# Moving the output writes of the last stage from POOL's DMA queue to SP's

## The reference

```python
xn = _layernorm(x, axis=-1)
x = x + _L0_attn_ref(xn, wq, wkv_a, wkv_b, wo) + _L0_ffn_ref(xn, router_w, gate_w, up_w, down_w)

def _L0_attn_ref(x, ...):            # 16 heads, 128 plain and 64 rotary columns
    ...
    attn = jax.nn.softmax(scores, axis=-1)
    o = jnp.einsum('bhqk,bkhd->bqhd', attn, v).reshape(b, s, H * VD)
    return o @ wo

def _L0_ffn_ref(x, ...):             # 16 experts of 768, the two best of each row count
    ...
    h = jax.nn.silu(g) * u
    expert_out = jnp.einsum('ebtf,efd->ebtd', h, down_w)
    out = jnp.einsum('ebtd,bte->btd', expert_out, combine)
    return out
```

## Time and profile before

| what | value |
|---|---|
| runs of the kernel before | 7406.59, 7946.9, 7163.06 us (median 7406.59) |
| the profiled execution | 7154.16 us |
| its span, slowest core (core 0) | 7152.6 us |
| spans of the 8 cores | 7116.0 to 7152.6 us |
| PE busy | 5868.2 us, 82% |
| DVE busy | 2477.7 us, 35% |
| POOL busy | 341.8 us, 5% |
| DMA queue q0 (POOL) | 490336 packets, 233.66 MB |
| DMA queue q1 (SP) | 19120 packets, 136.32 MB |

### The profile page before, as it was taken

One profiled execution on the slowest core, in us unless ns is written; L12 is line 12 of the kernel. 1 busy time (PEld: TensorE's weight loads), 2 busy tenths in 40 slices (PEclk: granted clock), 3 DMA queues, 4 the chain that ended last, 5 costly groups with the idle time before them and its releaser, 6 DMA issues.

```text
span 7152.6 us, 76524 instructions; the slowest of 8 cores (7116.0 to 7152.6 us)
## 1 busy us (share of the span) xinstructions
PE 5868.2 (82%) x28475; PEld 2792.7 (39%) x28992; DVE 2477.7 (35%) x4485; ACT 817.9 (11%) x1975; POOL 341.8 (5%) x377
## 2 busy tenths in 40 slices
PE   1677657777777778999999999999999999999900
PEld 1334323433343433444444444444444444444400
DVE  5445324554545443313322331332233123213334
ACT  2022102212221220000000000000000000000000
POOL 0000000000000000000000000000000000000000
PEclk9866676677667758999999999999999999999955
DMA  2311241022013105242233324233332423333165
GB/s 94 40 13 16 60 143 15 10 90 41 10 26 98 17 1 136 24 53 36 37 35 42 42 24 53 36 38 34 42 42 24 53 36 39 32 42 41 12 240 229
DMA packets 509816, 374.91 MB, mean 52 GB/s; under 512 B 468880, under 2 KB 470928, under 8 KB 486928
## 3 DMA queue, kind: packets, MB, share of 16 engines
q0 software_dynamic: 490336, 233.66, 24.2%
q1 hardware_dynamic: 19120, 136.32, 5.1%
HBM read 457.83 MB, written 83.89 MB: 76 GB/s over the span
## 4 chain that ended last, share of the span: by engine, by line
PE 75%; DVE 7%; DMA 6%; ACT 3%; issue 3%; ACTq 2%; DVEq 1%; POOL 0%; SPq 0%; POOLq 0%
PE psG L946 18%; PE psU L952 18%; PE psD L969 18%; PE psA L586 3%; PE psA L664 3%; DMA rb<-scr 3%; ACT probs L871 3%; PE psA L671 3%; PE psAV L701 2%; PE psAV L646 2%; PE psA L576 2%; ACTq L876 2%; PE psTa L633 2%; DMA xw<-x 2%; DVE colM L770 1%
## 5 line engine op out<-in xcount | busy, mean ns | idle before, releaser
L946 PE MATMUL psG<-xnT,gb 128*128 128x512 bf16 x6024 | 1381.5, 379 | 24.8 <-DMA ub<-uw 18.5
L952 PE MATMUL psU<-xnT,ub 128*128 128x512 bf16 x6022 | 1379.9, 379 | 6.4
L969 PE MATMUL psD<-db,hT 128*128 128x512 bf16 x6018 | 1324.4, 379 | 24.5 <-DVE hT L1007 16.9
L1007 DVE TENSOR_TENSOR hT<-sgt,psU 128x512 bf16<-128x512 f32 x384 | 264.1, 688 | 2407.3 <-PE psU L952 2407.3
L1021 DVE SCALAR_TENSOR_TENSOR acc<-psD,comb,acc 128x512 bf16<-128x512 f32 x960 | 721.2, 751 | 544.4 <-PE psD L969 544.4
L946 PEld LDWEIGHTS psG<-xnT,gb 128*128 128x128 bf16 x6144 | 601.4, 98 | 744.8 <-issue 21.0
L969 PEld LDWEIGHTS psD<-db,hT 128*128 128x128 bf16 x6144 | 596.4, 97 | 752.5 <-issue 201.1
L952 PEld LDWEIGHTS psU<-xnT,ub 128*128 128x128 bf16 x6144 | 601.2, 98 | 724.9
L994 ACT ACTIVATE sgt<-psG 128x512 f32<-128x512 f32 x384 | 229.3, 597 | 3680.0 <-PE psG L946 3679.9
L664 PE MATMUL psA<-kns,qn 128*128 128x512 bf16 (+3 forms) x560 | 249.5, 490 | 308.4 <-ACT probs L871 203.6
L871 ACT ACTIVATE probs<-psA,colD 128x512 bf16<-128x512 f32 (+3 forms) x640 | 391.6, 620 | 937.5 <-PE psAV L646 472.2
(11 more groups left out here) (135 smaller groups left out, 2980.5 us busy)
## 6 DMA issues: line engine op xcount, KB each, us to landing
scr<-stage SPq DMA_DIRECT2D x64, 1024.0 KB, 4.0
gb<-gw POOLq DMA_DIRECT2D x96, 512.0 KB, 6.3
ub<-uw POOLq DMA_DIRECT2D x96, 512.0 KB, 8.3
db<-dw POOLq DMA_DIRECT2D x16, 3072.0 KB, 19.5
rb<-scr SPq DMA_DIRECT2D x32, 1024.0 KB, 12.7
rb<-scr POOLq DMA_DIRECT2D x32, 1024.0 KB, 10.6
xbuf<-x SPq DMA_DIRECT2D x16, 1024.0 KB, 5.1
xw<-x SPq DMA_DIRECT2D x16, 1024.0 KB, 7.0
```

Source lines behind the costliest of these rows:

```text
L946: i = t.matmul(ps_g[:], gb[sl][:, dc * 128:(dc + 1) * 128], xnt(dc)[:, tb * 512:(tb + 1) * 512], start=(dc == 0), stop=(dc == ND - 1))
L952: i = t.matmul(ps_u[:], ub[sl][:, dc * 128:(dc + 1) * 128], xnt(dc)[:, tb * 512:(tb + 1) * 512], start=(dc == 0), stop=(dc == ND - 1))
L969: i = t.matmul(ps_d[:], hT[:, fc * 2048 + tc * 128: fc * 2048 + (tc + 1) * 128], db[:, fc * 2048 + dcol * 512: fc * 2048 + (dcol + 1) * 51 ...
L1007: i = v.tensor_tensor(out=hT[:, fc * 2048 + tb * 512: fc * 2048 + (tb + 1) * 512], in0=sgt[k % 2][:], in1=psU[k % 2][:], op=ALU.mult)
```

## The change

The output writes go from POOL's instruction stream to SP's. In SP's loop the write of tile tc - 1, with its wait for the last addition of that tile, stands in front of the loads of `rb[0]` and `rb[1]` for tile tc; the write of the last tile follows the loop, and SP and no longer POOL waits for the last two writes. In POOL's loop only the loads of `rb[2]` and `rb[3]` are left, each with its wait for the third addition of the tile before. VectorE's instructions, the buffers and the bytes moved are the same.

```diff
@@ SP @@
                     for tc in range(NT):
                         if tc >= 1:
+                            wait(sy, ("madd", tc - 1, 4))
+                            i = sy.dma_start(out[(tc - 1) * 128:tc * 128, :], ost[(tc - 1) % 2][:])
+                            sems[f"dOUT{(tc - 1) % 2}"].inc(i, 16)
+                            mark(("outw", tc - 1), sems[f"dOUT{(tc - 1) % 2}"])
+                        if tc >= 1:
                             wait(sy, ("madd", tc - 1, 0))
                         sy.dma_start(rb[0][:], scr[0][tc * 128:(tc + 1) * 128, :]).then_inc(
                             sems[f"dMRG{tc % 2}"].h, 16)
...
                         i = sy.dma_start(rb[1][:], scr[1][tc * 128:(tc + 1) * 128, :])
                         sems[f"dMRG{tc % 2}"].inc(i, 16)
                         mark(("mld", tc, 0), sems[f"dMRG{tc % 2}"])
+                    wait(sy, ("madd", NT - 1, 4))
+                    i = sy.dma_start(out[(NT - 1) * 128:NT * 128, :], ost[(NT - 1) % 2][:])
+                    sems[f"dOUT{(NT - 1) % 2}"].inc(i, 16)
+                    mark(("outw", NT - 1), sems[f"dOUT{(NT - 1) % 2}"])
+                    sy.wait_ge(sems["dOUT0"].h, sems["dOUT0"].n)
+                    sy.wait_ge(sems["dOUT1"].h, sems["dOUT1"].n)
 
@@ POOL @@
                         i = g.dma_start(rb[3][:], scr[3][tc * 128:(tc + 1) * 128, :])
                         sems["dMISC"].inc(i, 16)
                         mark(("gld", tc, 0), sems["dMISC"])
-                        wait(g, ("madd", tc, 4))
-                        i = g.dma_start(out[tc * 128:(tc + 1) * 128, :], ost[tc % 2][:])
-                        sems[f"dOUT{tc % 2}"].inc(i, 16)
-                        mark(("outw", tc), sems[f"dOUT{tc % 2}"])
-                    g.wait_ge(sems["dOUT0"].h, sems["dOUT0"].n)
-                    g.wait_ge(sems["dOUT1"].h, sems["dOUT1"].n)
```

## The result

The changed kernel is slower: 1.012 times the kernel before, with a 95% interval of 1.0093 to 1.0147, which is 67 to 105 us on 7154. The profiled execution took 7243.43 us, against 7154.16 before. The ratio leaves out executions in which the cores of a die ran at a lower clock than the others; the plain medians (7233.09 us of 9 executions, 7284.82 of 10 of the kernel before) contain some.

The account below looks back on a forecast made before the run. Bound taken: the merge's transfers and adds in series, 356.1 us. Losing SP's prefetch adds 14 steps by 1.3 us, 18 us, and 4.3 us for the fifteenth: 7154 + 22 = 7176 us, range 7138 to 7225.

Parts of the forecast that it names:

- The mechanism: In the merge, SP's loads of rb0/rb1 lose their one-tile prefetch, outweighing POOL's loads issued 3.0 us earlier: +22 us, chance 0.66.
- The transfer term: All five transfers of a merge tile, 5.24 MB, keep their measured 15.3 us early and 13.4 us late.
- The wake-up: In each merge tile, 0.1 us between the end of the transfer and the first add.
- A third reading: SP's queue takes about 2 us from issue to data when nothing else runs, read from the loads of tile 1.
- rival (c): In the merge, POOL's and SP's queues don't overlap: transfer 17.0 us a tile, +42 us, 7219 us; chance 0.09.
- A transfer of over 17 us: Sign that the forecast is wrong: a merge tile's transfer over 17 us, where 13.4 to 15.3 us were expected.
- The sum: 14 merge steps at 1.3 us, 18 us, plus 4.3 us for the fifteenth, end of kernel 0: +22 us, 7176 us.
- Its upper end: Queues that don't overlap at all, transfer 17.0 us in 16 tiles: 7219 us, with 6 us of margin 7225.
- The skill's rates: About 358 GB/s for each core of a streaming HBM pair, an estimated 14.6 us of transfer in all tiles.
- The 4 us in which SP's queue stayed behind a busy POOL queue: SP's queue starts 4.3 to 6.4 us after L1087's start, before POOL's runs dry at 7.2: no hole.

Follow-up runs that it names:

- e1_loads_first: Changed kernel with SP issuing the loads of rb0/rb1 first and the output write behind them; 0.9907 times the kernel before, profiled at 7083 us.
- e3_no_prefetch: Kernel before with SP's loads of rb0/rb1 waiting for the last add of the tile before, not the first; 1.0096 times the kernel before.
- e2b_pool_late: Changed kernel with POOL's loads of rb2/rb3 waiting for the last add of the tile before, not the third; 1.0034 times the kernel before.
- e4_no_writes: Changed kernel without the output writes of tiles 0 to 13, waits and loads otherwise as they were; profiled execution 7142.63 us.
- e5_sbuf_source: Changed kernel with the merge's loads of rb0 to rb3 reading pieces of xnT in SBUF instead of HBM; 1.0041 times the kernel before.
- e6_write_behind: Changed kernel with SP, still after the last add, issuing the loads of rb0/rb1 before the output write; 1.0019 times the kernel before.

## Why the prediction was right and wrong

**The mechanism.** Right. The prefetch is gone, all 16 first adds wait for rb0/rb1, the second add waits for nothing, POOL's issues start 0.37 us after the last add begins (0.42 forecast), and there is no short last step on core 2 (24.1 us). e1_loads_first and e3_no_prefetch, which give the prefetch back and take it alone, show that this and not the write's place is the cause.

**The tile.** Forecast for an undisturbed tile: 1.27 + 13.4 + 0.1 + 7.5 = 22.3 us. Measured on core 2: 1.4 + 14.5 + 1.2 + 7.3 = 24.4. Two terms were mis-sized by 1.1 us each, and these are the steps of the sum that failed for a core by itself.

The transfer term. I took "the measured 15.3 and 13.4, since those are the same 5.24 MB with the same kinds of packets on the same two queues". It was the order that was not the same. In the kernel before the write goes first and alone, and its slow stretch is about 2 us long (229 GB/s). In the changed kernel POOL's loads are under way when the write is issued, and the slow stretch is 5 us long at 303 GB/s. e2b_pool_late, where the write is first again, has 13.6 us from packet to packet against 14.6; e4_no_writes puts the price of the write behind POOL's loads at 3.8 us instead of 2.5.

The wake-up. I put 0.1 us between the end of the transfer and the add, and 1.2 were needed: 0.7 us in which the engines stop one after the other, and 0.5 us from the end of the last packet to the add (0.43 to 0.58 in all tiles of the changed kernel). In most tiles of the kernel before the value is hidden, since the pair that VectorE waited for was complete while other bytes still ran, and I read the end of that pair as the start of L1080. The last tile, in which SP's queue is silent, would have shown it: its last packet ends at 7135.60 and L1080 starts at 7136.13. The same error made rb2/rb3 look complete 0.9 to 1.3 us before the last byte in the earlier trace rows, when it was about 2.5 us (in the late tile 7117.28 and 7119.84). A tail of other bytes hides this delay; who takes the tail away must pay for it.

A third reading was off and did no harm to the sum. I let SP's queue take 2 us from issue to data. The records of that first tile have its first packets at 6813.42, 0.9 us after the issue; what came at 6814.4 was the full rate. And the first packet of POOL's queue comes 1.1 to 1.2 us after the issue, not 0.85.

By the last add, the 15 steps took 323.5 us before (6817.5 to 7141.0). On core 3 they took 363.3 us, +40, where +22 was forecast.

**The pairs.** Missed altogether, the sum has no term for them, and it is as large: 405.1 us on core 1, another +42. The prediction had the neighbour's effect in its rows, as the 15.3 us of the early tile against the 13.4 of the late one, and treated it as something that passes, because in the kernel before it does: steps of core 0 fall from 23.6 us to 20.9 within eight. In the changed kernel two of three pairs that collide stay at 26 to 29 us as long as both cores run, and in e3_no_prefetch three pairs end near 26. That the neighbour is what slows them is supported, not proved, by e5_sbuf_source (no long tile without loads from HBM) and by the last steps of cores 1 and 5. In rival (c), "queues in series", I had a transfer of 17.0 us, and core 0 has about that (17.6 from packet to packet), but from another cause: the head of its transfer is as fast as on core 2, the tail isn't. A transfer of over 17 us was one of my signs of being wrong, and on cores 0 and 4 it came.

**The sum.** 7154 + 40 + 42 - 5 + 13 = 7244, for 7243 measured. The 5 us are the end of the kernel: from the last write's issue to the end of the span it took 7143.87 to 7152.6 on POOL, 8.7 us, and takes 7237.70 to 7241.9 on SP, 4.2 us, of which I had counted 0; the same difference is there on all eight cores. The 13 us are the later start of the core that is now the slowest. In the kernel before, the 15 steps take 314.5 to 325.8 us and the cores differ by 11 us; in the changed kernel they take 363.3 to 405.7 and differ by 42, so that a late core in a colliding pair sets the time. A pair that doesn't collide ends at 7170.6 and 7182.5 us, around the 7176 that were forecast, but that is luck: its 15 steps are 40 us longer than those of the slowest core before and not 22, and it ends there because core 2 reached its first last add 18 us sooner than that core and saved 5 us at the end.

**The range.** Its upper end, 7219 us before the margin, had the transfer at 17.0 us, but the rest of the tile as in the sum. It would have had to hold both the wake-up and a transfer slowed by the neighbour in every tile.

**The skill's rates.** I had set the 358 GB/s that "DMA: Bandwidth & Descriptors" of the Trainium skill (Specifications and Bandwidth) gives each core of a busy pair against the rows, and put the transfer at an estimated 14.6 us by it. The undisturbed transfer is 14.5 us, but that is a coincidence of 303 and 421 GB/s in turn. The collided one of core 0 runs at 5.24 MB in 17.7 us, 296 GB/s, below the rule, with one write in five pieces.

**The 4 us in which SP's queue stayed behind a busy POOL queue** were real in both kernels (4.7 us in the tile of core 2). SP's first packet comes 7.0 us after the last add's start, later than the 4.3 to 6.4 of the forecast, and it was harmless, as forecast, because POOL's queue runs to 9.5 us or more: on core 2 the engines never run dry between 7020 and 7034.

**What stays open.** Why some pairs stay in each other's way to the end in the changed kernel and in e3_no_prefetch, but others (cores 6 and 7 here, and all in the kernel before and in e2b_pool_late) come apart, isn't settled. Without writes (e4_no_writes) and with the write behind the loads (e6_write_behind) no pair stands out. Open is also how a write whose packets haven't started slows the loads in front of it. Where two cores' transfers lie against each other can't be read from traces whose times each begin at the core's own first instruction, and no run here shifted one core of a pair against the other.

## What to carry to other kernels

Before a transfer is put in front of others on a queue, look at what its wait does to those behind it: here the write's wait for the last add took the loads' head start of a whole tile away, and the same write placed behind the loads makes the kernel 0.9% faster instead of 1.2% slower. When the last byte becomes the one that is waited for, count what lies between the end of full engines and the add, here 0.7 us of uneven end and 0.5 us behind the last packet, and not the value seen where other bytes still ran. And where two cores' transfers can disturb each other, size a transfer by the slower of the rates that the trace shows and for every step, unless something forces the cores apart.

## What the runs showed of the hardware

- 1.05 MB of writing to HBM, issued while POOL's loads from HBM ran, cost 3.8 us, and 4.19 MB of reads 10.7 us (the changed kernel and e4_no_writes, undisturbed cores): 1.4 times the price of the same bytes read. With the write first (e2b_pool_late) it cost 2.6 us (13.6 against 11.0 from packet to packet). The slow stretch, 303 GB/s, holds only packets of the loads; it is missing without the write (418 GB/s) and with the loads' sources in SBUF (413 GB/s).
- The second queue to get work has its first packet late while the first is busy: 4.7 us after the issue for SP's queue behind POOL's (core 2), 5.5 us for POOL's behind SP's (e2b_pool_late, core 4). With nothing else running it is 0.8 us for SP's queue (e2b_pool_late) and 1.2 us for POOL's (core 2).
- VectorE's add begins 0.43 to 0.58 us after the end of the last packet that it waits for, in all tiles of the changed kernel.
- In a colliding pair the two cores lose their 2.8 us in different ways: cores 0 and 4 in a tail (237 GB/s in one tile of core 0), cores 1 and 5 with first packets some 3.0 us after the issue and with an issue of a load on SP that takes 1.7 and 1.4 us in the median instead of 0.4. A long issue alone is no sign of it: with sources in SBUF it takes 1.2 us on all cores, and the tiles are short.
- A kernel whose last write is on POOL's queue ended 8.8 to 9.1 us after its issue, with the same write on SP's queue 4.2 to 4.4 us, on all eight cores.
- With sources in SBUF, 5.24 MB a tile take 22.4 us a tile on even cores and 22.9 to 23.3 on odd ones.
